# A memory layer that begins with two shared-memory groups, and takes over the last row scatters of the routing layer

## What is computed

```python
probs = softmax(x @ w_gate); rw, sel = top_k(probs, 2); rw = rw / rw.sum(-1)
tx = rows of x sorted by (sequence, memory), the last 1024 of each memory, missing ones zero
q, k, v = tx @ w_q * scale, tx @ w_k[m], tx @ w_v[m]
gk = log_sigmoid(tx @ w_gk1[m] @ w_gk2[m] + b_gk[m]) / 16
o_mem = gated_linear_attention(q, k, v, gk)      # a recurrence over the rows of each memory
o_rout = the rows of o_mem put back to their tokens, weighted by rw
o_sh = gated_linear_attention(x @ w_q * scale, x @ w_ks, x @ w_vs, gks)   # shared memory, over all tokens
o = rmsnorm(o_rout + o_sh) * silu(x @ w_g); return o @ w_o
```

## Time and profile before

| | us |
|---|---|
| median of 3 runs | 2499.81 (2498.53 to 2507.68) |
| the profiled execution | 2522.7 |
| its span | 2521.0 |
| mean granted clock of TensorE in it | 0.92 |
| busy: TensorE / VectorE / ScalarE / GpSimd | 2123.9 / 1816.8 / 1546.2 / 1521.3 |
| routing layer | about 1411.5 to 1554.4 |
| memory layer (`phase_gla`) | about 1554.4 to 2141.8 |

### The profile page before, as it was taken

One profiled execution on the slowest core, in us unless ns is written; L12 is line 12 of the kernel. 1 busy time (PEld: TensorE's weight loads), 2 busy tenths in 40 slices (PEclk: granted clock), 3 DMA queues, 4 the chain that ended last, 5 costly groups with the idle time before them and its releaser, 6 DMA issues. The chain is left out here.

```text
span 2521.0 us, 107266 instructions
## 1 busy us (share of the span) xinstructions
PE 2123.9 (84%) x43952; PEld 1629.8 (65%) x43952; DVE 1816.8 (72%) x4507; ACT 1546.2 (61%) x3824; POOL 1521.3 (60%) x3168
## 2 busy tenths in 40 slices
PE   8789999999999999988499443899999997876893
PEld 5557777777767777765378342677767765654782
DVE  6689999989989998846355552677777775764456
ACT  5578889988888988824233221566766664653330
POOL 3367778877878887885545365454445444356452
PEclk9989999999999999998799655899999998888896
DMA  6911111111121111134466443111111110733456
GB/s 214 281 53 43 47 48 47 43 50 43 46 76 50 43 43 50 24 127 164 114 216 208 165 159 118 31 52 50 54 49 51 43 35 30 250 147 115 143 149 227
DMA packets 188837, 245.65 MB, mean 97 GB/s; under 512 B 41673, under 2 KB 144982, under 8 KB 187457
## 3 DMA queue, kind: packets, MB, share of 16 engines
q1 hardware_dynamic: 161824, 182.08, 24.1%
q0 software_dynamic: 19872, 50.41, 5.9%
q10 hardware_dynamic: 6656, 6.31, 0.9%
HBM read 136.08 MB, written 106.50 MB: 96 GB/s over the span
## 5 line engine op out<-in xcount | busy, mean ns | idle before, releaser
L672 ACT ACTIVATE at_E<-at_S,at_mn 128x1024 f32<-128x1024 f32 (+7 forms) x704 | 592.1, 847 | 58.9 <-DVE at_mn L741 45.6
L741 DVE TENSOR_REDUCE at_mn<-at_S 128x1 f32<-128x1024 f32 (+3 forms) x448 | 484.5, 1100 | 6.2 <-PE at_S L851 5.8
L892 PE MATMUL at_pcs<-at_E,at_c 128*32 128x256 f32 (+1 forms) x4864 | 410.6, 339 | 2.5 <-issue 2.4
L851 PE MATMUL at_S<-am_sk,am_sq 96*32 96x512 bf16 (+3 forms) x4608 | 375.3, 348 | 9.3 <-ACT at_E L672 2.3
L609 POOL TENSOR_TENSOR at_kvo<-am_kh,am_vh 128x256 f32<-128x256 f32 x512 | 304.8, 629 | 0.1
L892 PEld LDWEIGHTS at_pcs<-at_E,at_c 128*32 128x32 f32 x4864 | 227.1, 109 | 27.1 <-issue 5.4
L1363 POOL DMA_INDIRECT expert_out<-m_ysb,m_dst x158 | 155.4, 984 | 133.7 <-issue 75.2
L594 POOL TENSOR_TENSOR at_half<-at_half 128x128 f32<-128x128 f32 (+4 forms) x640 | 185.5, 290 | 50.1
L662 ACT ACTIVATE at_Tt<-at_S,at_mn 128x192 f32<-128x192 f32 x512 | 174.1, 431 | 59.9 <-DVE at_mn L729 59.8
L851 PEld LDWEIGHTS at_S<-am_sk,am_sq 96*32 96x32 bf16 x4608 | 146.6, 97 | 81.1 <-ACT at_E L672 31.7
L892 PE MATMUL at_pcs<-at_Tt,at_c 128*32 128x128 f32 x1024 | 177.9, 275 | 0.9 <-issue 0.9
(11 more groups left out here) (393 smaller groups left out, 5711.6 us busy)
## 6 DMA issues: line engine op xcount, KB each, us to landing
m_xg<-expert_rows SPq DMA_DIRECT2D x158, 129.0 KB
am_sq<-q_parts SPq DMA_DIRECT2D x192, 64.0 KB, 2.4
am_sk<-k_parts SPq DMA_DIRECT2D x192, 64.0 KB, 2.3
memory_rows<-m_blank SPq DMA_DIRECT2D x16, 516.0 KB
gl_hx<-memory_rows SPq DMA_DIRECT2D x32, 258.0 KB, 4.5
m_wgu<-in_f_wgu SPq DMA_DIRECT2D x2, 4096.0 KB
rt_yin<-expert_out SPq DMA_DIRECT2D x7, 1024.0 KB, 12.3
fn_yin<-expert_out SPq DMA_DIRECT2D x7, 1024.0 KB, 8.1
```

Of the source, the lines that this page charges most:

```text
L672: ins = nc.scalar.activation(E[:, at:at + w], S[v % NS_B][:, i * CW:i * CW + w], ACT.Exp, bias=mn[:, q, s, 1 + j:2 + j], scale=-1.0, accum ...
L741: nc.vector.tensor_reduce(mn[:, q, :, :].rearrange("p s k -> p (s k)")[:, at[0]:at[0] + 1], S[v % NS_B][:, 0:w], AX.X, ALU.min).then_inc(s ...
L851: ins = nc.tensor.matmul(S[v % NS_B][x, at:at + cw], sq[:, u, t * P + x.start:t * P + x.stop], sk[:, u, c0 + c:c0 + c + cw], start=True, s ...
L892: ins = nc.tensor.matmul(pcs[j * R:(j + 1) * R, cols[0]:cols[1]].rearrange("p (b c) -> p b c", c=P), lhsT, rhs, start=(n, j) not in touche ...
```

## The change

The scatters of the last two routing steps (6 and 7, `LATE` = 2) are no longer issued by the routing layer. Their rows and slots live in buffers that outlast the phase (`late_rows`, `late_slot`), and so does the semaphore `sent`. The routing layer ends when 48 scatters have landed. In the memory layer GpSimd issues the eight of step 6 behind its constants and ahead of `decays(0)`, and the eight of step 7 behind `decays(0)`, ahead of the product of the output weights. The order of the groups is now a list: two shared groups first, then own groups of both sequences chunk by chunk, with a shared group behind the chunks 1 to 5 and one at the very end. SyncE loads turned rows for groups 0 and 1 first, then `later`, then waits for all 64 scatters, and only then loads own rows, into a ring that takes the place of `late_rows`.

```diff
-        hx = m.sb("hx", [P, NTT, XW])
+        NLATE = LATE * G
+        early_rows = m.sb("hx", [P, NTT - NLATE, XW])
...
+        def row_tiles(t0, t1):
+            return late_rows[:, t0:t1, :] if t0 < NLATE else early_rows[:, t0 - NLATE:t1 - NLATE, :]
...
-            sp.wait_ge(sent, NTT * TOPK * 16)
+            sp.wait_ge(sent, (NTT - NLATE) * TOPK * 16)
...
-            pool.tensor_copy(hx[:, :, D], tok_i[:, :]).then_inc(made, 1)
+            pool.tensor_copy(row_tiles(0, NLATE)[:, :, D], tok_i[:, 0:NLATE])
+            pool.tensor_copy(row_tiles(NLATE, NTT)[:, :, D], tok_i[:, NLATE:NTT]).then_inc(made, 1)
...
                 if n in (1, 3):
                     scale_of(n // 2 + 2)
+                if n >= NS - LATE:
+                    continue
...
-        hx = m.sb("hx", [P, NH, U, XW])
+        hx = late_rows[:, :, :].rearrange("p (n u) x -> p n u x", u=U)
...
+        GROUPS = [(B, 0), (B, 1)]
+        for s in range(NCHUNK):
+            GROUPS += [(b, s) for b in range(B)]
+            if 1 <= s < NCHUNK - 2:
+                GROUPS.append((B, s + 1))
+        GROUPS.append((B, NCHUNK - 1))
...
         def shared(a):
-            return a % (B + 1) == B
+            return GROUPS[a][0] == B
...
+            load_turned(0)
+            load_turned(1)
+            for to, src in later:
+                sp.dma_start(to, src).then_inc(later_in, 16)
+            sp.wait_ge(sent, NTT * TOPK * 16)
             for n in range(NH):
                 load(n)
-            for to, src in later:
-                sp.dma_start(to, src).then_inc(later_in, 16)
...
+            def scatter(n):
+                pool.wait_ge(sent, n * U * TOPK * 16)
+                for t in range(NTT - (n + 1) * U, NTT - n * U):
+                    for j in range(TOPK):
+                        pool.indirect_dma_start(out=gx, out_offset=bass.IndirectOffsetOnAxis(ap=late_slot[:, t, j:j + 1], axis=0),
+                                                in_=late_rows[:, t, :], in_offset=None, bounds_check=B * NM * CAP - 1,
+                                                oob_is_err=False).then_inc(sent, 16)
+
+            scatter(NTT // U - LATE)
             decays(0)
+            for n in range(NTT // U - LATE + 1, NTT // U):
+                scatter(n)
             pool.wait_ge(later_in, len(later) * 16)
...
-                    pe.wait_ge(turned[a % 2], (a // (B + 1) // 2 + 1) * 64)
+                    pe.wait_ge(turned[a % 2], turned_loads(a))
```

More of the change, by code:

```diff
@@ L1713, with phase_route @@
 GATE_NORM = 16.0
-def phase_route(nc, acc, tw_f, yb, w_gate, gx, hT_dram, tw_dram, weights, w_gk1t, w_gk2, w12):
+LATE = 2
+def phase_route(nc, acc, tw_f, yb, w_gate, gx, hT_dram, tw_dram, weights, w_gk1t, w_gk2, w12, late_rows, late_slot,
+                sent):
     with ExitStack() as ctx:
@@ L1765, in first_tile, with slot_tiles @@
             return NTT - (n + 1) * G
+        def row_tiles(t0, t1):
+            return late_rows[:, t0:t1, :] if t0 < NLATE else early_rows[:, t0 - NLATE:t1 - NLATE, :]
+        def slot_tiles(t0, t1):
+            return late_slot[:, t0:t1, :] if t0 < NLATE else early_slot[:, t0 - NLATE:t1 - NLATE, :]
         @block.sync
@@ L2042, in _, with phase_gla @@
                     low_rank()
-def phase_gla(nc, gx, hT_dram, wq, wk, wv, w12, bg, yb, o_dram, ident, later, won, wo, nw):
+def phase_gla(nc, gx, hT_dram, wq, wk, wv, w12, bg, yb, o_dram, ident, later, won, wo, nw, late_rows, late_slot, sent):
     with ExitStack() as ctx:
         m = Mem(nc, ctx, "gl_")
+        m.sems.append(sent)
         U = 4
@@ L2108, in phase_gla, with turned_loads @@
         block = ctx.enter_context(nc.Block())
+        GROUPS = [(B, 0), (B, 1)]
[4 more added lines that the diff above has]
+        GROUPS.append((B, NCHUNK - 1))
+        OWNS = [a for a in range(NG) if GROUPS[a][0] < B]
+        NOWN = len(OWNS)
         def shared(a):
-            return a % (B + 1) == B
+            return GROUPS[a][0] == B
         def own(a):
-            return a - a // (B + 1)
-        NOWN = own(NG)
+            return sum(x < a for x in OWNS)
+        def turned_loads(a):
+            return sum(64 for x in range(a % 2, a + 1, 2) if shared(x))
         def mem(a, u):
@@ L2121, in chain_of @@
         def chain_of(a, u):
-            return B * NM + u % B if shared(a) else a % (B + 1) * NM + u
+            return B * NM + u % B if shared(a) else GROUPS[a][0] * NM + u
         def sent_before(pair, kind):
@@ L3011, in build @@
             wq, wk = early("wq", [P, KC, P]), early("wk", [P, MS, KC, P])
+            late_rows = early("late_rows", [P, 3 * 4, XW])
+            late_slot = kept.enter_context(nc.sbuf_tensor("ready_late_slot", [P, LATE * 4, TOPK], U32))
+            sent = nc.alloc_semaphore("ready_sent")
             wv, w12, bg = early("wv", [P, MS, KC, D]), early("w12", [P, MS, KC, P]), early("bg", [P, MS])
@@ L3014, in build @@
                        (bg[:, :], a["b_bias"]))
-            phase_route(nc, Y, tw, yb, a["b_gate"], gx, hT_dram, tw_dram, weights, a["b_gk1t"], a["b_gk2"], w12)
+            phase_route(nc, Y, tw, yb, a["b_gate"], gx, hT_dram, tw_dram, weights, a["b_gk1t"], a["b_gk2"], w12,
+                        late_rows, late_slot, sent)
             later = [(wo[:, :, :], a["b_wo"]), (nw[:, :], a["b_norm"]), (wg[:, :, :], a["b_wg"]),
@@ L3019, in build @@
                 later.append((hT[:, n, :, :], hT_dram[:, :, n * 4 * P:(n + 1) * 4 * P].rearrange("k p t -> p k t")))
-            phase_gla(nc, gx, hT_dram, wq, wk, wv, w12, bg, yb, o_dram, ident, later, won, wo, nw)
+            phase_gla(nc, gx, hT_dram, wq, wk, wv, w12, bg, yb, o_dram, ident, later, won, wo, nw, late_rows,
+                      late_slot, sent)
         hx = tile("rows", [P, NTT, XW])
```

26 lines of the change are left out of this document (13 added, 13 removed).

## The result

| | before | after |
|---|---|---|
| median, us | 2500.5 (4 runs, 2498.5 to 2507.7) | 2470.1 (4 runs, 2468.6 to 2471.1) |
| ratio | | 0.988, interval 0.9867 to 0.9894 |
| profiled execution / its span | 2522.7 / 2521.0 | 2469.6 / 2467.9 |

The changed kernel is 30.4 us faster; 24.2 were forecast. The forecast 2475.6 is 5.5 us too high and the range, 2470 to 2487, holds the result at its very edge. The bounds of the prediction's terms gave at most 29 us; the result lies beyond them, and inside the range only through the microsecond that was added for the runs' scatter. That much of the hit is luck.

The account below looks back on a forecast made before the run. TensorE was taken to bound the full pipeline, with gains at the routing layer's tail and the memory layer's filling. 23.1 - 0.2 + 4.0 - 0.5 - 2.2 = 24.2 us off 2499.8 gives 2475.6, range 2470 to 2487.

Parts of the forecast that it names:

- the two stretches: The tail of the routing layer and the filling of the memory layer's pipeline, where the change was to act.
- Part 1: End of the routing layer: with sixteen of 64 scatters gone, the memory layer starts 23.1 us earlier, bounds 20.7 to 24.2.
- (a): GpSimd's last remaining scatter ends the routing layer: memory layer starts at 1529.1 to 1530.2, at most 24.2 us gained.
- (b): SyncE's store of the routing weights at 1527.96 ends the routing layer: memory layer starts 3.35 us later, at 1531.3.
- I carry 24.2 us over unscaled: The summed gain from the profile, 24.2 us, is taken unscaled off the runs' median of 2499.8, giving 2475.6.
- Part 2: Filling of the memory layer with two shared groups, first late scatters hidden: 4.0 us gained, bounds 2.0 and 4.9.
- Part 3: Second late scatter group, behind the first decays: state spread hidden, own rows with 0.7 us slack; 0.5 us charged, bounds 0 and 4.
- Part 4: Memory layer's loop: two own groups' transposes move into the full, TensorE-bound pipeline; 2.2 us lost, bounds 0 and 4.
- Rival 1: Filling gives part back, by late own-row loads or a longer low clock: gain 18 us, time 2482; chance 0.22.
- rival 2: The memory layer's TensorE-bound loop gets less clock: gain 12 us, time 2488; chance 0.08.
- the prediction's signs: Right: memory layer starts about 3.4 us after the store. Wrong: loop's clock or group length changed over 0.1 us a group.
- Rival 3: GpSimd starved beside VectorE in the filling: gain gone at 1.5 us a scatter; at 2.0, time 2508; chance 0.04.

Follow-up runs that it names:

- e1: The kernel before, run again unchanged for a second profile; 2504.42 us in one run.
- e2: Kernel before with only the new order of groups, all 64 scatters in the routing layer; 2495.65 us, ratio 0.9978.
- e9: The changed kernel run again unchanged beside the kernel before on one chip; 2468.09 us, ratio 0.9881.
- e11: Changed kernel with the low-rank product moved to the end of the routing layer; 2467.13 us, ratio 0.9875 to the kernel before.
- e12: Changed kernel with the moves of e5 and e11 together; 2497.32 us, ratio 0.9917 to the kernel before.
- e5: Changed kernel with the product of the output weights moved behind the decays of group 1; 2503.93 us, ratio 0.9948 to the kernel before.
- e6: e5 with the first state spread also moved ahead of both late scatter groups; 2508.2 us, ratio 0.9953 to the kernel before.
- e7: Changed kernel with the old order of groups and both late scatter groups ahead of the first decays; 2531.47 us, ratio 1.0051 to the kernel before.
- e8: Changed kernel with three late scatter groups, one ahead of the first decays and two behind; 2512.94 us, ratio 0.9981 to the kernel before.
- e10: e5's kernel run again on the same chip as e9; 2468.63 us, ratio 0.988 to the kernel before.
- e4: Changed kernel with both late scatter groups ahead of the first decays; 2475.34 us, ratio 0.9898 to the kernel before.

## Why the prediction was right, step by step

**Direction and mechanism: right.** The time came from the two stretches that the prediction named. Against e1, the trace of before of the matching kind: routing layer 144.8 to 116.6, 28.2 us; S to kt1 63.2 to 60.2, 3.1 us. The rest (a loop that was 3.6 us shorter here, but equal in e2 and e9, a last group 1.5 us longer, and 2.0 us less in the phases behind it) is what two traces differ by anyway. 31.3 us of these two against 30.4 by the medians.

**Part 1, the term that was mis-sized.** Forecast 23.1 us, measured 28.2. The failed step is the choice between (a) and (b): "S = 1531.3, later than (a), so I take it". The store that decided there came late only in the trace that was read. On the kind of chip on which both medians were taken it is issued 110.0 us after the layer's start (1516.80 less 1406.80) and has landed after 1.5 us by its line's view, 5.1 us before S; e11 had it 0.9 us earlier in the layer, and the layer wasn't shorter. By the scatters the 28.2 are accounted for: the last early scatter now stands in for one 25.1 us later (1518.45 to 1543.57 in e1), it comes 1.5 us earlier in its layer, and the wait behind it is 4.87 us, not 6.51. Bound (a), 24.2 us, didn't hold it, for two reasons: it took the 7.65 us of the layer before and not the 6.51 of its own rows, by which it would have been 25.4, and it couldn't know that this wait would fall to 4.87. On the second kind of chip the choice was right in four traces of five (e12 is open): in e5, e6, e7 and e8 S follows the store by 2.60 us each time, against the 3.35 taken, and the routing layer of e5 to e7 is 118.9 to 120.7 us where the forecast gives 119.8 (1531.3 less 1411.5) plus 0.2. So the arithmetic held for the trace from which it came, and the step "I carry 24.2 us over unscaled" to a median of another kind was where 5 us were lost. It also hid an error of the other sign: on the second kind the filling gains nothing. S to kt1 is 68.6 us in e5 and 63.7 in e12, where the trace read has 63.5 and 60.0 was forecast. The forecast of 24.2 would have been about 10 us too much in e5 (14.3) and near in e12 (23.0).

**Part 2, the filling: right within 1.5 us at each point.** First product at S + 4.6 (forecast 5.4); zb at 1531.71, S + 8.3 (9.4, though 5.4 and the 3.8 from rows make 9.2); the base of group 0 done at 1541.81, S + 18.4 (19.4); decays held by the scatters, begun at S + 20.4 (19.8) and so 2.0 us after their data where 0.3 was forecast; gate of group 1 at S + 22.8 (24.1). The order alone gained 4.6 us in e2, where "Fill: 4.0 us gained" stood.

**Part 3: right in sum, wrong in place.** A loss of 0.5 us was charged to the own rows, which came in time. "Hidden, with 2 us to spare" fell: TensorE waited 1.76 us for the state spread, because it reached its first output at S + 39.6, 2.3 us before the forecast, and the first spread was done only at S + 41.2, 1.4 us behind it. e2 and the changed kernel differ by 1.5 us from S to kt1, e9 and e10 by 1.9: that is what the second group costs. It could be moved away (e10) but is too small to be measured in the whole. e4 agrees that the first group is hidden: with decays 13.1 us later TensorE waited 8.59 us for them, so the first 4.5 us of such a delay cost nothing.

**Part 4: not seen.** "2.2 us lost" was charged for transposes in the full pipeline; e2 has 491.1 us from kt1 to kt23 and e1 491.0. The groups follow each other in mostly 21.7 to 22.5 us whether own or shared, which the transposes' 1.09 us doesn't move. Over 491 us of that stretch TensorE was busy for 457.48 us in e2 and for 455.96 in e1: it does 1.5 us more work there and stands that much less. What it would have waited for instead wasn't tried.

**The rivals.** Rival 1 (own rows late, low clock longer) and rival 2 (less clock: 1.00 in the loop) didn't occur in the changed kernel's run. Two of the prediction's signs came out against it all the same. S came 6.6 us after the store, not 3.4, as told above. And the loop's length per group changed by more than a tenth of a microsecond, which was to mean wrong: kt1 to kt23 is 504.8 in the trace read and 487.4 here, 0.8 us a group, and the loop's clock went from 0.98 to 1.00. That isn't the change's doing, since e1, the kernel before, has 491.0 at a clock of 0.99. It is the difference between the two kinds again.

Rival 3, starved GpSimd, is refuted: its threshold was 1.5 us on each scatter. The sixteen took 17.4 us together:

```profile
L2281 POOL DMA_INDIRECT memory_rows<-ready_late_rows,ready_late_slot x16 | 17.4, 1085 | 5.2 <-issue 4.4 <-POOL gl_hmask L2229 0.8
```

That is 1.085 us each against 0.97 in the routing layer, 0.12 more. Three of sixteen took 1.39 to 1.64 us; all three ran beside VectorE. The one at 1555.20 overlaps its scan and the one at 1558.43 its product `gl_r`:

```profile
1554.82 1.22 DVE L2459 TENSOR_TENSOR_SCAN gl_c<-gl_restart,gl_g 128x512 f32<-128x512 f32 x1
...
1558.28 0.68 DVE L2467 TENSOR_TENSOR gl_r<-gl_c 128x512 f32<-128x512 f32 x1
```

But eight others ran beside VectorE too and took 0.98 to 1.04 us. In e7 all sixteen ran while VectorE stood idle, and none took over 1.03. So VectorE's work beside a scatter goes with a delay, of few of them; which of its operations does it isn't shown.

The page "SBUF — State Buffer" of the Trainium skill, section "SBUF: two separate sides", names operations in a two-port mode, an fp32 copy for one, as what holds up a GpSimd-issued DMA. In direction the trace agrees. It doesn't show that cause: the slow scatter of 1.44 us had only a scan and a `scalar_tensor_tensor` of VectorE beside it. The size that the prediction took from the page, an estimate of 2.5 us on each, isn't borne out: the most was 0.67 us, on one in sixteen, and the estimate of 2515 us missed by 45.

## What to carry to other kernels

Transfers at the end of a layer can move into the start of the next if that start has work that doesn't need them: the move alone cost 13 us (e7), the reordering alone gained 5 (e2), both together 30. Split the moved work by what each piece may delay, and stop when something else (here a store) holds the end. Before a profile is used for absolute terms, look whether it is of the same kind as the runs: the profiled execution stood 0.9% above the median, its store stood 5 us later in the layer than in a profile near the median, that store was chosen as what ends the changed layer, and 5 us went wrong by that.

## What the runs showed of the hardware that was not expected

Two kinds of chip (or moments, as said above), some 20 us apart for the same kernel before (2498.8 and 2500.5; 2518.2 and 2520.4), and a change that gains 30 us on one kind and, in versions that differ by parts that cost nothing there (e5, e12), 14 to 23 on the other. On the second kind TensorE's small products are separated by waits for nothing that the profile shows, 46 to 53 of them in the memory layer of e5, e6, e8 and e12, against 6 to 15 in the eight traces of the first kind; the trace of before that was read has 37 and e7 33. They fall into two parts. In the filling e5, e6, e8 and e12 have 9 to 16, all but one of each beside GpSimd's scatters. The trace of before has two there, and e7 none, where the scatters are over before the first scores. From kt1 to kt23 there are no scatters, and all six traces of this kind have 33 to 37, before and e7 included, 19 to 25 of each beside one of GpSimd's sends. They make 13.8 to 15.8 us together, against 3.0 to 6.1 on the first kind, and that is most of the 11 to 18 us by which these loops are longer than e1's. The kernel before has this second part as well, so it can't explain a smaller gain; the first part can.

That the scatters cause the first part isn't shown. It rests on coincidence in time in four traces, and the changed kernel itself didn't run on such a chip.

The wait between the last scatter of a layer and the next layer fell with the number of scatters: 6.51 and 6.62 us with 64, 5.52 with 56, 4.87 to 5.06 with 48 where the scatters held the end (6.14 on the chip of e12). The landing of the last scatter isn't what changed: it took 2.5 us in e1 (64), the changed kernel and e11 (48) alike. The time from there to the next layer did, from 5.0 us to 3.3 and 3.4. Nothing tried says why.
